# Graph network in one kernel: in stage two each eighth edge group, not each sixteenth, takes its fourth quarter from columns in SBUF instead of a gather

## The chip, the cores and the metric

One Trainium2 chip, one of its NeuronCores. The metric is the device time of one execution in microseconds (us); for the kernel before it is the median of three runs.

## The reference, cut to what matters

Two graph layers run over the same 200,000 edges (sorted by target `dst`) and 6,250 nodes of 128 features. The change lies in the second, an attention layer with 4 heads of 32 features:

```python
h = relu(layernorm(x))
x_l = (h @ W_l.T + b_l).reshape(n, 4, 32)
x_r = (h @ W_r.T + b_r).reshape(n, 4, 32)
z = leaky_relu(x_l[src] + x_r[dst], 0.2)
e = einsum('ehc,hc->eh', z, att)
e = exp(e - segment_max(e, dst)[dst])
alpha = e / (segment_sum(e, dst)[dst] + 1e-16)
out = segment_sum(alpha[:, :, None] * x_l[src], dst)
x = x + elu(out.reshape(n, 128) + bias)
```

Every edge needs the row `x_l[src]`. `dst` is sorted, `src` is random, so these rows have to be fetched one by one.

## The kernel before, in words

The edges are cut into 391 groups of 512 (`EG`), a group into four quarters of 128 edges (`J = 4`). Stage one (the message network, function `edges_mlp`) runs over all groups, then stage two (`edges_attention`) does. Each is a software pipeline written out by hand, with no scheduler: the five engines have programs of their own, tied by semaphores, and all go through the same slots. Eight slots are a round (`U = 8`), and slot g works at once on several groups of different age.

In slot g of stage two:

- TensorE turns the weights of group g-4 (L2466), multiplies the scores of g-2 (L2471, waits for `t_zt`), adds up the denominators of g-5 (L2476, L2477, wait for VectorE's `t_own_x`), then makes `z` of g-1 (L2496 for the target half, L2499 for the four quarters of source rows), and the weighted sum of g-4 (L2511, waits for ScalarE's `t_a_edge`).
- VectorE, in this order: its part of the columns (L931 loads the row numbers into registers, L935 copies), `t_zt` of g-2 (L2615), `t_own_x` of g-5 (L2620, waits for L2511 of the slot before), the logits of g-3 (L2627), `t_gap` and `t_drop` of g-5 (L2646 to L2653, wait for L2477 of this slot), the mask of g (L2663), and the accumulation of g-5 (L2669 to L2675, waits for ScalarE's `t_shrink`). Once a round come a few operations of a finished node tile, a reciprocal (L2180) among them.
- ScalarE: `t_a_edge` of g-4 (L2530, waits for L2466), `t_a_row` of g-3 (L2538), `t_shrink` (L2544), its part of the columns (L931, L2554), then `t_z` and `t_pen` of g-1 (L2558, L2560).
- GpSimd (POOL in the profile) issues the gathers, indirect DMAs of 128 rows from the table `tab_l` in HBM into `t_ring`, one a quarter (`gather_groups`, L1014). Before the gathers of group g it waits for TensorE: the first for the weighted sum of g-8, the next three for the turned weights, the `z` and the scores of groups some 4 to 7 back, all of which TensorE does near slot g-3. So GpSimd stays about four groups ahead of TensorE, and can't run further.
- SyncE loads the target windows and rows, and single rows for the lone groups.

Two kinds of group need no fourth gather. In each 32nd group (`lone`, g % 32 = 31) SyncE loads the 128 rows one by one, four a slot. In each 16th group (`chosen`, g % SPAN = 3, from g = 2 * SPAN on: 35, 51, ... 387, that is 23 groups) the rows come from `r.left`, the source features of all nodes, which lie transposed in SBUF. VectorE and ScalarE copy them a column at a time, 8 a slot (`CHOSEN = P // SPAN`), over the 16 slots that end two slots before slot g: four a slot by VectorE (`CHOSEN_BY_VECTOR`), the other four by ScalarE. SyncE fetches the list of row numbers ahead (`fetch_chosen`, L948). TensorE adds the 128 columns to `z` by a plain product with the identity (L2502, in place of a transpose), and turns them once more (L2495), from where ScalarE copies them to rows (L2537) for the weighted sum.

```python
    n, i = (g + SPAN - 2) // SPAN, (g - 2) % SPAN
    ...
    first += i * CHOSEN
    ...
    for q in range(many):
        last = move(r.chosen[n % 2][:, first + q:first + q + 1], r.left[:, bass.ds(rows[q], 1)])
```

Stage one has the same device under other names (`pick_columns`, L907, L911, L1750): there each eighth group has columns, eight a slot by either engine.

Of the kernel before, what the change touches and what calls it, by code (L numbers as in the profile page):

```python
# [32 lines left out]
PICKED = P // U  # L33
BY_VECTOR = 8
SOONER = 2
SPAN = 16
CHOSEN = P // SPAN
CHOSEN_BY_VECTOR = 4
LEAD = 5
SCALED = 2  # L40
FRONT = 2
# [7 lines left out]
def after(eng, sem, count):  # L49

    if isinstance(count, int) and count <= 0:
        return
    eng.wait_ge(sem, count)
# [12 lines left out]
def before(rnd, slot, k, tail):  # L66


    if tail and slot - k >= tail:
        return None  # L70
    slot -= k
    while slot < 0:
        slot += U
        rnd = rnd - 1
    if isinstance(rnd, int) and rnd < 0:
        return None
    return rnd, slot
# [804 lines left out]
def column(k, r, g, j):  # L882
# [3 lines left out]
    if j == J - 1 and chosen(k, g):  # L886
        return r.chosen_rows[g // SPAN % 2][:]
    return r.got[g % U][:, j, :]
# [26 lines left out]
def chosen(k, g):  # L915

    return g % SPAN == 3 and 2 * SPAN <= g < k.groups - 1


def choose_columns(nc, eng, k, r, s, g, first, many, move, done):  # L920

    n, i = (g + SPAN - 2) // SPAN, (g - 2) % SPAN
    if not many or not chosen(k, n * SPAN + 3):
        return
    if i == 0:
        if n == 2:
            eng.wait_ge(r.s_turned, 1)
        eng.wait_ge(r.s_chosen_ids, 16 * (n - 1))
        after(eng, s["t_zp"], (n - 2) * SPAN + 4 if n > 3 else 0)
    first += i * CHOSEN  # L930
    _, rows = nc.values_load_multi_w_load_instructions(  # L931
        r.chosen_ids[n % 2][:, first:first + many], engines=[eng.engine], min_val=0, max_val=k.N - 1,
        skip_runtime_bounds_check_because="src names rows of the node features, as the gathers take it")
    for q in range(many):
        last = move(r.chosen[n % 2][:, first + q:first + q + 1], r.left[:, bass.ds(rows[q], 1)])  # L935
    last.then_inc(done, 1)
# [1175 lines left out]
def edges_attention(nc, t, k, sems):  # L2112
# [3 lines left out]
    with ExitStack() as ctx:  # L2116
# [406 lines left out]
        def fast_scalar(act):  # L2523
            act.wait_ge(s["t_tiny"], 1)
            def body(rnd, slots, tail):
                for u in slots:
# [25 lines left out]
                    if not tail:  # L2552
                        choose_columns(nc, act, k, r, s, rnd * U + u, CHOSEN_BY_VECTOR, CHOSEN - CHOSEN_BY_VECTOR,
                                       lambda out, col: act.activation(out, col, ACT.Copy), r.s_chosen_s)  # L2554
# [19 lines left out]
        def fast_vector(dve):  # L2574
# [14 lines left out]
            def body(rnd, slots, tail):  # L2589
                for u in slots:  # L2590
# [19 lines left out]
                    if not tail:  # L2610
                        choose_columns(nc, dve, k, r, s, rnd * U + u, 0, CHOSEN_BY_VECTOR, dve.tensor_copy, r.s_chosen_v)
                    if at := before(rnd, u, 2, tail):
# [116 lines left out]
```

## Time and profile before

| | |
|---|---|
| median of 3 runs | 4867.06 us (4866.64 to 4870.92) |
| the profiled execution | 4868.36 us, span of its instructions 4865.6 us |
| stage one, about | 0 to 2430 us of the span |
| stage two, about | 2430 us to the end |
| busy, share of the span | PE 73%, PEld 57%, DVE 52%, ACT 46%, POOL 60% |
| mean granted TensorE clock | 0.79 of full speed |

A row of the timeline gives an instruction's start and duration, what it writes and reads, and in brackets how long its engine had been idle and what ended that. "remote" is a wait whose end the profile can't put down to an instruction, "issue" time in which the engine waited for nothing that the profile shows. PE is TensorE's matmul, PEld its weight load, DVE is VectorE, ACT ScalarE, POOL GpSimd; DVEq and ACTq are the instructions of their sequencers, as the loads of registers. A busy share is no bound by itself: no engine of this kernel is busy all the time, and what sets the length of a slot has to be read from the waits.

### The profile page before, as it was taken

Reading aid. Unit: us, or ns where it says so; the run is one execution under the profiler, and the core shown is the slowest. Engines: PE = TensorE matmul, PEld = TensorE weight load, DVE = VectorE, ACT = ScalarE, POOL = GpSimd, SP = SyncE. Lnnn points to the kernel's source line nnn. Section 1 sums busy time; section 2 is a strip of 40 time slices with the busy share of each in tenths; the row PEclk is TensorE's granted clock in tenths of the full one; section 3 lists DMA queues with packets and bytes.
Section 4 is the critical chain, followed back from the end, with each engine's and each line's share of the span. In section 5 each row is a group of like instructions: output and inputs, shape, how many; then the busy total and the mean of one; then the engine's idle time right before and its main releaser. Section 6 shows DMA issues by size and latency. Waiting matters only on the chain.

```text
span 4865.6 us, 90325 instructions
## 1 busy us (share of the span) xinstructions
PE 3546.4 (73%) x21208; PEld 2770.5 (57%) x21208; DVE 2514.7 (52%) x12768; ACT 2249.2 (46%) x8862; POOL 2910.5 (60%) x3098
## 2 busy tenths in 40 slices
PE   4778777888777778777757767667666666766766
PEld 3666666666666666666645555555545555555554
DVE  3444444444444444444436566666565665666665
ACT  3343444444444444444335555555555555555555
POOL 5666666666666666666466656666555665566564
PEclk7676767666766776777778889898898999889888
DMA  5344444444444444444322222222222222222221
GB/s 152 112 112 116 114 113 113 114 116 116 114 116 111 114 115 114 114 118 113 87 77 73 72 71 72 72 72 70 71 71 70 72 72 71 71 72 70 74 71 46
DMA packets 361802, 450.21 MB, mean 93 GB/s; under 512 B 163461, under 2 KB 217827, under 8 KB 361263
## 3 DMA queue, kind: packets, MB, share of 16 engines
q1 hardware_dynamic: 263359, 244.49, 17.6%
q0 software_dynamic: 97504, 199.69, 16.1%
q8 instruction: 174, 2.85, 0.2%
q14 instruction: 365, 2.99, 0.2%
q10 hardware_dynamic: 400, 0.20, 0.0%
HBM read 420.79 MB, written 23.28 MB: 91 GB/s over the span
## 4 chain that ended last, share of the span: by engine, by line
another core or an unknown queue 32%; DVE 23%; PE 20%; issue 14%; ACT 6%; DVEq 4%; DMA 0%; ACTq 0%; SPq 0%; POOL 0%; POOLq 0%
PE bank L2471 4%; DVE t_zt L2615 3%; DVE lone L911 3%; PE bank L2511 3%; PE bank L1694 3%; DVE m_pre L1793 2%; DVE t_logit L2627 2%; DVEq L907 2%; DVE t_chosen L935 2%; PE bank L2477 1%; PE bank L2499 1%; ACT t_a_row L2538 1%; PE bank L2466 1%; PE bank L2476 1%
## 5 line engine op out<-in xcount | busy, mean ns | idle before, releaser
L1014 POOL DMA_INDIRECT t_ring<-tab_l,src_t x1530 | 1446.1, 945 | 983.9 <-remote 447.3
L1014 POOL DMA_INDIRECT m_ring<-tab_a,src_t x1517 | 1440.3, 949 | 921.0 <-issue 387.3
L1694 PE MATMUL bank<-w,m_attr_t 128*128 128x128 f32 x3128 | 854.2, 399 | 128.1 <-issue 100.4
L1793 DVE TENSOR_TENSOR m_pre<-bank,m_ring 128x512 f32<-128x512 f32 (+1 forms) x391 | 264.0, 675 | 1168.4 <-remote 1078.3
L2471 PE MATMUL bank<-t_zt,att_wn 128*128 128x512 f32 x782 | 495.7, 719 | 499.3 <-issue 305.7
L1694 PEld LDWEIGHTS bank<-w,m_attr_t 128*128 128x128 f32 x3128 | 717.7, 280 | 233.3 <-issue 181.0
L1732 ACT ACTIVATE m_hid<-m_pre 128x512 f32<-128x512 f32 x391 | 245.8, 629 | 938.9 <-issue 663.7
L2530 ACT ACTIVATE t_a_edge<-bank 128x512 f32<-128x512 f32 x391 | 232.5, 595 | 699.4 <-remote 620.1
L2511 PE MATMUL bank<-t_ring,t_a_edge 128*128 128x128 f32 x3060 | 487.1, 310 | 64.6 <-issue 58.4
L2511 PEld LDWEIGHTS bank<-t_ring,t_a_edge 128*128 128x128 f32 x3060 | 448.3, 225 | 81.2 <-issue 73.9
L2471 PEld LDWEIGHTS bank<-t_zt,att_wn 128*128 128x128 f32 x782 | 132.7, 213 | 582.4 <-issue 359.2
L1699 PE MATMUL bank<-m_win,m_hot_t 96*128 96x128 bf16 x1564 | 430.5, 275 | 45.2 <-issue 44.9
L1682 PE MATMUL bank<-ident,m_ring 128*128 128x128 f32 x1564 | 363.1, 360 | 100.9 <-issue 90.8
L2476 PEld LDWEIGHTS bank<-diag_w,t_t_own_x 128*128 128x128 f32 x782 | 156.1, 218 | 446.7 <-issue 234.9
L1748 ACT ACTIVATE m_attr_t<-bank 128x512 f32<-128x512 f32 x391 | 230.2, 589 | 342.3 <-remote 264.6
L1662 PE MATMUL bank<-m_hid,m_hot 128*32 128x129 f32 x3128 | 208.1, 348 | 209.6 <-ACT m_hid L1732 119.1
L1682 PEld LDWEIGHTS bank<-ident,m_ring 128*128 128x128 f32 x1564 | 274.5, 196 | 126.6 <-issue 114.0
L2538 ACT ACTIVATE t_a_row<-t_logit,t_den_max 128x512 f32<-128x512 f32 x391 | 281.2, 719 | 104.9 <-DVE t_den_max L2627 73.3
L1750 ACT ACTIVATE lone<-HT 128x1 f32 x3008 | 323.3, 195 | 10.2 <-issue 3.5
L2615 DVE TENSOR_TENSOR t_zt<-bank,t_z 128x512 f32<-128x512 f32 x391 | 266.6, 682 | 51.7 <-issue 31.1
L2646 DVE TENSOR_TENSOR t_gap<-bank,HT 128x32 f32<-128x32 f32 x391 | 74.5, 191 | 408.7 <-PE bank L2477 194.4
L911 DVE COPY lone<-HT 128x1 f32 x3008 | 277.5, 145 | 8.2 <-issue 7.5
(276 smaller groups left out, 6756.1 us busy)
## 6 DMA issues: line engine op xcount, KB each, us to landing
m_ring<-in_edge_attr_dram SPq DMA_DIRECT2D x390, 256.0 KB
t_rows<-dst_rows SPq DMA_DIRECT2D x196, 256.0 KB
m_rows<-dst_rows SPq DMA_DIRECT2D x196, 192.0 KB
t_ring<-tab_l,src_t POOLq DMA_INDIRECT x1530
m_ring<-tab_a,src_t POOLq DMA_INDIRECT x1517
lone<-tab_l SPq DMA_DIRECT2D x1408, 0.5 KB
m_win<-tab_b SPq DMA_DIRECT2D x391, 24.0 KB
t_win<-tab_r SPq DMA_DIRECT2D x391, 24.0 KB
```

What stands on the lines that cost most here:

```text
L911: last = move(k.lone[:, n % 2, first + q:first + q + 1], k.HT[:, bass.ds(rows[q], 1)])
L1014: pool.indirect_dma_start(out=r.got[u][0:rows, j, :], out_offset=None, in_=table, in_offset=bass.IndirectOffsetOnAxis(ap=k.src_t[0:rows, g ...
L1682: last = pe.transpose(p_attr[u % 2][:, j * P:(j + 1) * P], attr[u][:, j, :], k.ident[:])
L1694: pe.matmul(p_hid[q % 2][:, e], lhsT=attr_t[q % 2][:, e], rhs=k.w1[:, 2, :], start=True, stop=False)
L1699: last = pe.matmul(p_hid[q % 2][:, e], lhsT=hot_t[q % 2][0:3 * W, e], rhs=r.win[q][:], start=False, stop=True)
L1732: act.activation(hid[q % 2][:, :, 0:P], pre[q % 2][:].rearrange("p (j d) -> p j d", d=P), ACT.Relu).then_inc(s["m_h"], 1)
L1750: lambda out, col: act.activation(out, col, ACT.Copy), s["m_picked_s"])
L1793: last = dve.tensor_tensor(pre[q % 2][:, 0:some], p_hid[q % 2][:, 0:some], r.got[q].rearrange("p j d -> p (j d)")[:, 0:some], ALU.add)
L2471: pe.matmul(p_e[q % 2][:], lhsT=k.att_wn[:], rhs=zt[q % 2][:], start=True, stop=True).then_inc(s["t_ep"], 1)
L2511: last = pe.matmul(p_nd[q % 2][:, 3 * W:3 * W + P], lhsT=a_edge[q % 2][:, j, :], rhs=column(k, r, g, j), start=(j == 0), stop=(j == J - 1))
L2538: act.activation(a_row[q % 2][:], logit[q % 2][:], ACT.Exp, scale=-1.0, bias=den_max[q % 4][:, 1:2], accum_out=den_max[q % 4][:, 0:1]).the ...
L2615: dve.tensor_tensor(zt[q % 2][:], p_z[q % 2][:], z02[q % 2][:], ALU.max).then_inc(s["t_z"], 1)
```

## The change

Two constants. `SPAN` goes from 16 to 8, so `CHOSEN`, the columns a slot, from 8 to 16, and VectorE's part from 4 to 7, ScalarE's from 4 to 9.

```diff
-SPAN = 16
+SPAN = 8
 CHOSEN = P // SPAN
-CHOSEN_BY_VECTOR = 4
+CHOSEN_BY_VECTOR = 7
```

The chosen groups are now 19, 27, ... 387, that is 47 of them, one in every round from round 2 on. The columns of one group are made over the 8 slots that end two slots before its own, so the slots that carry columns are 10 to 385 (376 slots), where they were 18 to 385 (368 slots). The two buffers of columns, of rows and of row numbers take turns as before, and SyncE fetches a list each 8 slots instead of each 16.

VectorE in stage two, in a slot that already had columns (t_chosen is the buffer of columns, X the features in SBUF, L935 ISA a register operation that goes with each copy, t_zt what TensorE's scores wait for):

```order
 L935 ISA
 L935 COPY t_chosen<-X 128x1
+L935 ISA
+L935 COPY t_chosen<-X 128x1
+L935 ISA
+L935 COPY t_chosen<-X 128x1
+L935 ISA
+L935 COPY t_chosen<-X 128x1
 L2615 TENSOR_TENSOR t_zt<-bank,t_z 128x512
 L2620 TENSOR_TENSOR t_t_own_x<-bank,same_head 128x128
```

Three more copies stand in each such slot ahead of `t_zt` and `t_own_x`, on which TensorE waits. ScalarE has five more at the like place, ahead of `t_z`.

TensorE in the slot that makes `z` of group 19, the first of the 24 groups that are new among the chosen ones. A group with four gathers, as group 19 was before:

```order
L2477 MATMUL bank<-t_cd,same_head 128x64
L2496 MATMUL bank<-t_hot_t,t_win 128x512
L2499 MATMUL bank<-ident,t_ring 128x128 x4
L2511 MATMUL bank<-t_ring,t_a_edge 128x128 x4
L2466 MATMUL bank<-ident,t_a_row 128x128 x4
```

and in the changed kernel:

```order
L2477 MATMUL bank<-t_cd,same_head 128x64
L2495 MATMUL bank<-ident,t_chosen 128x128
L2496 MATMUL bank<-t_hot_t,t_win 128x512
L2499 MATMUL bank<-ident,t_ring 128x128 x3
L2502 MATMUL bank<-t_chosen,ident 128x128
L2511 MATMUL bank<-t_ring,t_a_edge 128x128 x4
L2466 MATMUL bank<-ident,t_a_row 128x128 x4
```

One transpose of gathered rows has become a product with the columns, and one turn of the columns is added; the order is otherwise the same.

GpSimd's whole program for stage two, the difference (a row stands for so many gathers):

```order
 L1014 DMA m_ring<-tab_a,src_t 80x128 x4
-L1014 DMA t_ring<-tab_l,src_t 128x128 x1526
+L1014 DMA t_ring<-tab_l,src_t 128x128 x1502
 L1014 DMA t_ring<-tab_l,src_t 80x128 x4
```

24 gathers are gone, and nothing else has moved there.

## Rows read from the trace of the kernel before

**Rows 1.** Timeline of stage two, one slot with three gathers, all engines; start us, us

```profile
3037.74 0.29 DVE L2620 TENSOR_TENSOR t_t_own_x<-bank,same_head 128x128 f32<-128x128 f32 x1 [1.56 <-remote]
3037.80 0.60 ACT L2530 ACTIVATE t_a_edge<-bank 128x512 f32<-128x512 f32 x1 [2.13 <-remote]
3037.98 0.94 POOL L1014 DMA_INDIRECT t_ring<-tab_l,src_t  x1 [1.41 <-remote]
...
3038.88 0.19 DVE L2646 TENSOR_TENSOR t_gap<-bank,HT 128x32 f32<-128x32 f32 x1
...
3039.24 1.06 PE L2511 MATMUL bank<-t_ring,t_a_edge 128*128 128x128 f32 x8
...
3039.90 0.49 ACT L2554 ACTIVATE t_chosen<-X 128x1 f32 x4 [0.17 <-issue]
...
3040.13 0.60 PE L2466 MATMUL bank<-ident,t_a_row 128*128 128x128 f32 x4
...
3040.47 0.94 POOL L1014 DMA_INDIRECT t_ring<-tab_l,src_t  x1 [0.30 <-issue]
3040.74 0.50 DVE L935 COPY t_chosen<-X 128x1 f32 x4 [0.27 <-issue]
...
3041.15 0.68 DVE L2615 TENSOR_TENSOR t_zt<-bank,t_z 128x512 f32<-128x512 f32 x1
...
3042.70 0.29 DVE L2620 TENSOR_TENSOR t_t_own_x<-bank,same_head 128x128 f32<-128x128 f32 x1 [0.86 <-remote]
...
3042.93 0.94 POOL L1014 DMA_INDIRECT t_ring<-tab_l,src_t  x1 [1.51 <-remote]
```

**Rows 2.** Groups of instructions by line, 2550 to 4800 us; busy us, mean ns, idle before

```profile
L1014 POOL DMA_INDIRECT t_ring<-tab_l,src_t x1434 | 1355.5, 945 | 894.9 <-remote 426.7 <-issue 340.9 <-PE bank L2499 86.9
L2620 DVE TENSOR_TENSOR t_t_own_x<-bank,same_head 128x128 f32<-128x128 f32 x367 | 105.1, 286 | 313.1 <-remote 303.9 <-PE bank L2511 5.3 <-issue 3.2
L2646 DVE TENSOR_TENSOR t_gap<-bank,HT 128x32 f32<-128x32 f32 x367 | 69.9, 191 | 375.8 <-PE bank L2477 180.8 <-PE bank L2511 79.7 <-issue 72.2
```

**Rows 3.** Stretches, ten rounds of 32 gathers, first and sum; length, POOL busy

```profile
2693.20:2742.80 49.60, 29.33 (x32) 0.87 0.26 71
...
sum 502.20, POOL 303.83; mean POOL 30.38
```

**Rows 4.** Stretches, ten rounds each of the two kinds with one chosen group; sums

```profile
sum 487.00, POOL 288.15; mean POOL 28.82
...
sum 492.30, POOL 297.77; mean POOL 29.78
```

**Rows 5.** Instructions of single lines: columns, register loads, gathers; ns min/median/max

```profile
L935 DVE COPY t_chosen<-X x1472: 94/154/156, 2555.8 to 4808.9; 128x1 f32 x184
...
L931 DVEq TENSOR_LOAD <-w x192: 341/346/498, 2555.4 to 4808.1; - x192
L931 ACTq TENSOR_LOAD <-w x192: 306/311/358, 2561.2 to 4813.2; - x192
...
L907 DVEq TENSOR_LOAD <-wr x192: 593/596/812, 118.0 to 2375.6; - x192
L907 ACTq TENSOR_LOAD <-wr x192: 543/548/826, 122.0 to 2375.8; - x192
...
L1014 POOL DMA_INDIRECT t_ring<-tab_l,src_t x1500: 938/944/1076, 2449.6 to 4799.1; - x188
```

**Rows 6.** Stretches, three early rounds of 32 gathers: first and sum

```profile
2496.00:2545.50 49.50, 30.71 (x33) 0.84 0.27 70
...
sum 148.10, POOL 91.69; mean POOL 30.57
```

**Rows 7.** Timeline of DVE in stage two, where nothing is held

```profile
3018.15 0.68 DVE L2615 TENSOR_TENSOR t_zt<-bank,t_z 128x512 f32<-128x512 f32 x1
...
3020.53 0.19 DVE L2646 TENSOR_TENSOR t_gap<-bank,HT 128x32 f32<-128x32 f32 x1 [0.54 <-PE bank L2477]
```

## The prediction

> **What bounds the kernel now.** I read the page first (no engine is busy over 73% of the span, so no share names the bound), then the groups by line of stage two, then the timeline of single slots, then the lengths of whole rounds.
>
> In the groups by line, look at what stands behind each bar. GpSimd is busy 1355.5 us with 1434 gathers and idle 894.9 us; VectorE waits 313.1 us ahead of `t_own_x` and 375.8 us ahead of `t_gap` [rows 2]. All of them wait, and the rows name TensorE or nobody. The timeline shows how [rows 1]. `t_own_x` at 3042.70, and the next group's first gather at 3042.93, start within 0.25 us of one another, and at 3037.74, 3037.80 and 3037.98 they do so with ScalarE's `t_a_edge` too. What they wait for are matmuls of L2511 and L2466, which in this slot start at 3039.24 and 3040.13 and by their rows are over at 3040.30 and 3040.73. Yet nobody goes on until 3042.70, 2.2 us after the last gather of the group began at 3040.47. So TensorE's results, whose ends in a profile are only modelled, reach the others here when GpSimd has been quiet for a while. Whatever the cause, the slot has the shape: the gathers of a group at one pace, then one wait of everybody.
>
> The pace: a gather takes 0.945 us [rows 2] and the next follows 0.30 us later [rows 1], so 1.245 us. The wait: 1355.5 + 894.9 = 2250.4 us for 1434 gathers [rows 2], less 1434 x 1.245 = 1785, leaves 465 us over 367 slots, 1.27 us a slot. A slot of four gathers is then 4 x 1.245 + 1.27 = 6.25 us, one of three 5.0; the slot of the timeline, 3037.98 to 3042.93, took 4.95 [rows 1]. That is the main reading: **the number of gathers sets the length of a slot**, though their data are there long before they are needed.
>
> Whole rounds say it again. Ten rounds of 32 gathers took 502.2 us [rows 3], ten with one chosen group 487.0 and ten of the other kind with one 492.3 [rows 4]: 50.22 against a mean of 48.97, so 1.25 us for one gather less. In that difference the extra work of a chosen group (L2495, L2502, L2537) is paid already.
>
> **What it removes.** 24 gathers, at 1.245 us of pace each: 24 x 1.245 = 30 us, all on the path if the reading above holds. The rounds give 24 x 1.25 = 30 too. The added turns, products and copies to rows of the 24 new chosen groups are inside that number.
>
> **What it adds to VectorE.** Three copies a slot. Four take 0.50 us as a block [rows 1] and one 0.154 us [rows 5], so each further one adds (0.50 - 0.154) / 3 = 0.115, three 0.35 us. The load of row numbers is 346 ns for four and 596 ns for the eight of stage one [rows 5], so 63 ns a number, 0.19 us more, of which the engine sees all, since it already sits idle 0.27 us ahead of the block [rows 1]. Together 0.54 us a slot, and 376 x 0.54 = 203 us in all. The eight slots that had no columns get the whole block, some 1.4 us each, in rounds that are priced with the others.
>
> **What it adds to ScalarE.** Five copies at (0.49 - 0.19) / 3 = 0.10, 0.50 us, and five more numbers at (548 - 311) / 4 = 59 ns, 0.30 us [rows 1, 5]: up to 0.80 us a slot. It hides behind ScalarE's idle time ahead of `t_a_edge` (2.13 us at 3037.80) [rows 1]; what comes later by it is `t_z`, which VectorE takes a slot later. Priced at nothing; if the cover were gone, `t_a_edge` and with it L2511 would be late by up to 0.8 us.
>
> **What it adds elsewhere.** SyncE issues 24 more small fetches of numbers, and before each waits for the columns of the list before last, with the window loads of the next slots queued behind. It runs seven slots ahead of TensorE, and the columns it asks for are those of about the slot that TensorE is in, so this is a wait of under a slot against a lead of seven: nothing.
>
> **How much of VectorE's 0.54 us shows.** VectorE's chain runs through TensorE and back: `t_gap` at 3038.88 to the end of `t_zt` at 3041.83 is 2.95 us [rows 1]; from an end of `t_zt` (3018.83) to `t_gap` (3020.53) it is 1.70 where nothing is held [rows 7]. A slot of the chain alone is 4.65 us, with the change 5.19. Against 6.25 that hides; against a slot of three gathers, 4.95 to 5.0, it sticks out by some 0.2 us, and such slots will be 58 (47 chosen and 11 lone). Bounds: nothing, and all of it, 203 us. The nearest rows between are the early rounds of 32 gathers: the first, still without columns, took 49.5 us, the three together 148.1, so the two that have them 49.3 each [rows 6]. The later ones, with columns and the work on node tiles, took 50.22 [rows 3]. So 4 + 4 columns a slot, 8 x (0.50 + 0.27) = 6.2 us of VectorE a round, cost between nothing and 0.72 us a round, under 12% of what they take. At the same share the new 8 x 0.54 = 4.3 us a round cost 0 to 0.5 us, over 47 rounds 0 to 24. I take the middle, **12 us**; the 58 short slots at 0.2 us make the same.
>
> **The sum**: -30 + 12 = -18 us. The profiled execution took 4868.4 us, so 4850.4; the median of the runs is 1.3 us under it, so I forecast 4849.
>
> **A rule that speaks against it.** The copies of columns overlap gathers: the four from 3040.74 on lie inside the gather that began at 3040.47, and that one still took 0.94 us; over 1500 gathers the median is 944 and the longest 1076 ns [rows 5]. So the copies don't hold GpSimd up. The Trainium skill (SBUF — State Buffer, section "SBUF: two separate sides") states the opposite case: a VectorE copy of fp32 from SBUF to SBUF takes the port pair it shares with GpSimd, and the gather's descriptors can't be written meanwhile. By that rule each added copy would block a gather.
>
> **Rivals.**
>
> 1. *All of it hides.* For it: the early rounds, where columns cost nothing. Against: the short slots. Then -30: 4837 us. Chance 0.17.
> 2. *It cancels.* If the short slots are set by VectorE's chain with tile work in it (0.5 us instead of 0.2 in all 58, 29 us), the gathers' gain is given back: 4867 us, no change. Chance 0.15.
> 3. *Slower: a late result misses its gap.* TensorE's results get through when no gather is under way. In the short slot of each round, where the chain (5.19 us) is now longer than three gathers and the wait (5.0), L2511 or L2466 can come after GpSimd has started its next gather, and is then held for the length of one more, 1.245 us. Once a round that is 47 x 1.245 = 59 us, so -30 + 59 = +29: 4896 us. For it: the waits ahead of `t_gap` show that single results are held even now. Against: 0.2 us is little to miss by, and a slot late by that has a full slot of 6.25 us behind it to recover in. It decides from the point where 24 of the 47 rounds are hit. Chance 0.18.
> 4. *The copies block GpSimd after all.* Three copies of 0.154 us in 376 slots, one after the other on the gathers' path, are 174 us, so +144: 5011 us. Against it the rows above. Chance 0.02.
>
> That the change doesn't do what it says can be left out: the gathers in GpSimd's program went from 1526 to 1502.
>
> **How the numbers follow.** My forecast has 0.48. Single measurements of this kernel tell about 0.2%, 10 us, from no change. Of the forecast's own spread (0 to 24 us of cost around 12, so 4837 to 4861) some 0.07 falls inside 10 us of no change. Faster: 0.41 + 0.17 = 0.58. Same: 0.07 + 0.15 = 0.22. Slower: 0.18 + 0.02 = 0.20. The range takes in full hiding with a few us to spare, 4833, and reaches into rival 3 with fewer rounds hit, 4885; beyond it lie the rest of rival 3, rival 4 and a little on the fast side, some 0.2. The likeliest case alone has 4837 to 4861.
>
> **What would show it.** Gathers in stage two 1506 (1530 before), copies on L935 2632 (1472 before), on L2554 3384. Rounds with one chosen group of about 49 to 49.5 us, and none left at 50.2; slots of three gathers 5.0 to 5.5 us. The idle time ahead of `t_own_x` and `t_gap` should be less by some 0.5 us a slot in all, since the copies eat it; GpSimd's wait should stay near 1.27 us a slot. Wrong would be: rounds with a chosen group no shorter than 50 (rival 2 or 3), with GpSimd's wait grown to 1.5 us a slot and more, or gathers longer than 0.95 us in the mean (rival 4). If the rounds are 49.0 as before, rival 1 holds.

## The result and the profile after

The changed kernel takes **5189.69 us** (median of 4 runs, 5184.25 to 5191.47) against 4866.85 us (4 runs). The ratio is 1.0662, with an interval of 1.0645 to 1.0679: 323 us slower, where 18 us faster was forecast. The profiled execution took 5189.53 us, with a span of 5187.7 us. The whole loss lies in stage two: its first gather starts at 2432.6 us of the span, and at 2433.2 before.

The counts are the forecast ones: 1506 gathers in stage two, 2632 copies on L935, 3384 on L2554. The single lines show what is not. The columns are instruction, count, then minimum, median and maximum in ns, then first and last start:

```profile
L935 DVE COPY t_chosen<-X x2632: 153/154/156, 2507.2 to 5128.2; 128x1 f32 x188
...
L931 DVEq TENSOR_LOAD <-w x192: 1030/1040/1100, 2506.0 to 5126.3; - x192
L931 ACTq TENSOR_LOAD <-w x192: 1947/1959/2099, 2510.9 to 5133.6; - x192
...
L907 DVEq TENSOR_LOAD <-wr x192: 593/597/753, 118.6 to 2375.4; - x192
L907 ACTq TENSOR_LOAD <-wr x192: 537/548/857, 121.2 to 2375.6; - x192
```

VectorE's load of seven numbers takes 1040 ns and ScalarE's of nine 1959, where four took 346 and 311 [rows 5]. Yet eight numbers, in stage one of the same kernel, still take 597 and 548. Seven cost more than eight.

The groups by line of stage two, 2550 to 4800 us as in [rows 2]. In the kernel before, ScalarE's `t_a_edge` had this row:

```profile
L2530 ACT ACTIVATE t_a_edge<-bank 128x512 f32<-128x512 f32 x367 | 218.3, 595 | 667.0 <-remote 595.9 <-PE bank L2466 58.1 <-issue 12.7
```

and in the changed kernel:

```profile
L1014 POOL DMA_INDIRECT t_ring<-tab_l,src_t x1238 | 1171.6, 946 | 1079.6 <-PE bank L2499 667.6 <-issue 297.3 <-PE bank L2502 93.9
...
L2554 ACT ACTIVATE t_chosen<-X 128x1 f32 x2889 | 319.8, 193 | 574.4 <-issue 574.4
...
L2530 ACT ACTIVATE t_a_edge<-bank 128x512 f32<-128x512 f32 x322 | 188.8, 586 | 0.4 <-remote 0.4
...
L2620 DVE TENSOR_TENSOR t_t_own_x<-bank,same_head 128x128 f32<-128x128 f32 x322 | 90.4, 281 | 0.2 <-remote 0.2
...
L2646 DVE TENSOR_TENSOR t_gap<-bank,HT 128x32 f32<-128x32 f32 x322 | 61.7, 192 | 357.7 <-PE bank L2477 271.4 <-issue 84.0 <-PE bank L2511 2.3
```

2250 us now hold 322 slots, 6.99 us each, and not 367 of 6.13 [rows 2]. The 0.86 us times 376 slots are 323 us, the whole loss. GpSimd's wait, reckoned as in the prediction, is (1171.6 + 1079.6 - 1238 x 1.246) / 322 = 2.20 us a slot and not 1.27; it has a name now, L2499, TensorE's `z`, so GpSimd waits for a late TensorE. The wait ahead of `t_own_x`, 313.1 us before, is gone, and so is ScalarE's ahead of `t_a_edge`: 0.4 us, where it was 667.0. ScalarE instead waits 574.4 us ahead of its columns, for "issue", that is for its own sequencer, which is loading registers. The gathers' mean is 0.946 us, as before.

Ten rounds with one chosen group each, first and sum. The columns are the length of the stretch, the busy us (and count) of PE, PEld, DVE, ACT and POOL, then the granted clock, the DMA share and GB/s:

```profile
2737.98:2794.31 56.33, 35.25 (x200) 27.40 (x200) 33.27 (x172) 30.58 (x127) 29.32 (x31) 0.89 0.24 63
...
sum 568.84, PE 365.06 PEld 282.74 DVE 328.32 ACT 302.30 POOL 291.42; mean PE 36.51 PEld 28.27 DVE 32.83 ACT 30.23 POOL 29.14
```

56.9 us a round, against 48.7 and 49.2 [rows 4], with the same number of gathers. The timeline of one slot shows why (start, duration, engine; the idle time before it in brackets):

```profile
3036.60 0.58 ACT L2558 ACTIVATE t_z<-bank 128x512 f32<-128x512 f32 x1
...
3037.21 0.69 DVE L2615 TENSOR_TENSOR t_zt<-bank,t_z 128x512 f32<-128x512 f32 x1
...
3037.96 1.12 PE L2471 MATMUL bank<-t_zt,att_wn 128*128 128x512 f32 x2 [2.91 <-issue]
...
3039.06 0.41 PE L2477 MATMUL bank<-t_cd,same_head 128*128 128x64 f32 x2
...
3039.61 0.19 DVE L2646 TENSOR_TENSOR t_gap<-bank,HT 128x32 f32<-128x32 f32 x1 [0.76 <-issue]
...
3040.13 0.26 ACT L2544 ACTIVATE t_shrink<-t_drop 128x64 f32<-128x64 f32 x1 [0.58 <-DVE t_drop L2653]
3040.40 0.95 POOL L1014 DMA_INDIRECT t_ring<-tab_l,src_t  x1 [1.72 <-PE bank L2499]
...
3042.08 0.84 DVE L935 COPY t_chosen<-X 128x1 f32 x7 [0.95 <-issue]
3042.20 0.98 ACT L2554 ACTIVATE t_chosen<-X 128x1 f32 x9 [1.81 <-issue]
...
3043.09 0.58 ACT L2558 ACTIVATE t_z<-bank 128x512 f32<-128x512 f32 x1
...
3043.70 0.69 DVE L2615 TENSOR_TENSOR t_zt<-bank,t_z 128x512 f32<-128x512 f32 x1 [0.79 <-ACT t_z L2558]
```

Read it as a ring, a closed chain of waits that sets the length of a slot, from `t_z` to `t_z`: to `t_zt` 0.61 us, to L2471 0.75, to L2477 behind it in TensorE's order 1.10, to `t_gap` 0.55, to `t_shrink` 0.52, then ScalarE's load, up to its first column, 2.07, and its columns 0.89. That is 6.49 us from 3036.60 to 3043.09, and no gather stands in it. It is one of the shortest slots: from `t_zt` to `t_zt` those between 2800 and 3400 us take 6.48 us and more, in the mean 7.1; in the longer ones more comes on top (work on node tiles, a lower granted clock), which was not taken apart. Before, in the slot of [rows 1]:

```profile
3039.47 0.26 ACT L2544 ACTIVATE t_shrink<-t_drop 128x64 f32<-128x64 f32 x1
...
3040.30 0.58 ACT L2558 ACTIVATE t_z<-bank 128x512 f32<-128x512 f32 x1
```

So `t_shrink` to the first column (3039.90 [rows 1]) took 0.43 us, and the columns 0.40. The two last terms grew by 2.1 us, of which the old common wait of 1.27 us took up a part, and 0.86 us came out at the end.

### The profile page after: what moved, and what is told of

It reads as the page before. It is cut to its first block, busy times and chain, and to the rows that moved or that the text cites. A ratio compares the mean times of both kernels' runs of the same rounds, so it can differ in the third digit from the quotient of the medians.

```text
span 5187.7 us, 96749 instructions
## 1 busy us (share of the span) xinstructions
PE 3622.0 (70%) x21256; PEld 2874.7 (55%) x21256; DVE 2664.8 (51%) x13928; ACT 2442.5 (47%) x10798; POOL 2893.4 (56%) x3074
## 4 chain that ended last, share of the span: by engine, by line
PE 32%; issue 23%; another core or an unknown queue 21%; DVE 15%; DVEq 4%; ACT 4%; ACTq 1%; DMA 0%; SPq 0%; POOL 0%
PE bank L2471 9%; PE bank L2511 5%; PE bank L1694 3%; DVE lone L911 3%; PE bank L2499 3%; PE bank L2477 2%; PE bank L2466 2%; DVE m_pre L1793 2%; DVE t_zt L2615 2%; DVEq L907 1%; DVEq L931 1%; PE bank L2496 1%; PE bank L2476 1%; ACTq L931 1%
## 5 line engine op out<-in xcount | busy, mean ns | idle before, releaser
L1014 POOL DMA_INDIRECT t_ring<-tab_l,src_t x1506 | 1425.4, 946 | 1324.5 <-PE bank L2499 780.6
L2471 PE MATMUL bank<-t_zt,att_wn 128*128 128x512 f32 x782 | 532.1, 768 | 979.7 <-issue 727.4
L2471 PEld LDWEIGHTS bank<-t_zt,att_wn 128*128 128x128 f32 x782 | 133.4, 214 | 1076.5 <-issue 793.1
L2554 ACT ACTIVATE t_chosen<-X 128x1 f32 x3384 | 374.8, 193 | 673.7 <-issue 673.7
L2511 PE MATMUL bank<-t_ring,t_a_edge 128*128 128x128 f32 x3012 | 506.3, 323 | 3.9 <-ACT t_a_edge L2530 2.3
L935 DVE COPY t_chosen<-X 128x1 f32 x2632 | 317.6, 154 | 324.3 <-issue 319.8
L2511 PEld LDWEIGHTS bank<-t_ring,t_a_edge 128*128 128x128 f32 x3012 | 477.4, 240 | 4.8 <-ACT t_a_edge L2530 2.7
L2476 PEld LDWEIGHTS bank<-diag_w,t_t_own_x 128*128 128x128 f32 x782 | 179.2, 230 | 244.6 <-issue 238.1
```

The lines of the kernel that those rows point to most:

```text
L1014: pool.indirect_dma_start(out=r.got[u][0:rows, j, :], out_offset=None, in_=table, in_offset=bass.IndirectOffsetOnAxis(ap=k.src_t[0:rows, g ...
L2471: pe.matmul(p_e[q % 2][:], lhsT=k.att_wn[:], rhs=zt[q % 2][:], start=True, stop=True).then_inc(s["t_ep"], 1)
L2511: last = pe.matmul(p_nd[q % 2][:, 3 * W:3 * W + P], lhsT=a_edge[q % 2][:, j, :], rhs=column(k, r, g, j), start=(j == 0), stop=(j == J - 1))
```

## The experiments

The kernel before takes a very different time on different chips: 4802 us on the chip of e1 to e4 (mean granted clock of TensorE 0.80), 3910 on that of e5 to e8, 3911 on that of e9 to e12, 3917 for e13 to e16 (all three 0.89), 4858 for e17 and e18 (0.79). So each result is a ratio to the kernel before on the same chip. Where a difference is taken across chips, the text says so; e5 to e8 and e9 to e12 are such a case, with 0.3 us between their kernels before.

### e1: what a register load costs

The kernel before, with another length and first place of the load in each of the 16 slots between two chosen groups:

```diff
-    _, rows = nc.values_load_multi_w_load_instructions(
-        r.chosen_ids[n % 2][:, first:first + many], ...
+    if vector is True and i == 0:
+        _, rows = nc.values_load_multi_w_load_instructions(ids[:, first - 0:first + 4], ...
+    elif vector is True and i == 1:
+        _, rows = nc.values_load_multi_w_load_instructions(ids[:, first - 0:first + 5], ...
...
+    elif vector is True and i == 12:
+        _, rows = nc.values_load_multi_w_load_instructions(ids[:, first - 1:first + 7], ...
```

> The kernel before (each sixteenth group, four and four columns), but in stage two each slot's register load on VectorE and on ScalarE has another length and first place: on VectorE 4 to 14 and 16 numbers from a place divisible by eight, and 8, 8, 8 and 7 numbers from places that are not; on ScalarE 4 to 10, 12 and 13 numbers from places 0, 1, 4 or 7 of eight. Only the numbers that were used before are used. Theory A (the load's time follows the count of numbers in steps, and not in a straight line): 4 and 8 numbers take some 0.33 and 0.57 us wherever they start, 7 and 9 numbers some 1.04 and 1.96 us. Theory B (the place of the first number decides): 7 and 9 numbers from a place divisible by four take below 0.7 us, 8 numbers from place 1, 6 or 7 take over 1 us. The prediction's straight line (about 60 ns a number) would have 7 at 0.52 and 9 at 0.65 us, whatever the place. The run's own time should be some per cent above the kernel before by A, about the same by the straight line.

Measured: 4882.9 us in a single run against 4801.8, 1.7% more. In order: VectorE with 4, 5, 7, 8, 9, 12 and 16 numbers from a place divisible by eight, 8 from place 4, 7 and 8 from place 7; then ScalarE with nine from place 0, nine from place 7 (what the change does), and nine from place 4.

```profile
L934 DVEq TENSOR_LOAD <-w x12: 346/352/355, 2533.5 to 4730.2; - x12
L937 DVEq TENSOR_LOAD <-w x12: 601/608/612, 2540.8 to 4737.0; - x12
L943 DVEq TENSOR_LOAD <-w x12: 1030/1040/1050, 2553.0 to 4748.2; - x12
L946 DVEq TENSOR_LOAD <-w x12: 601/606/611, 2558.4 to 4753.9; - x12
L949 DVEq TENSOR_LOAD <-w x12: 851/853/856, 2566.0 to 4761.0; - x12
L958 DVEq TENSOR_LOAD <-w x12: 853/856/892, 2583.9 to 4780.5; - x12
L967 DVEq TENSOR_LOAD <-w x12: 1104/1108/1116, 2603.7 to 4797.6; - x12
L973 DVEq TENSOR_LOAD <-w x12: 594/596/601, 2616.4 to 4809.5; - x12
L976 DVEq TENSOR_LOAD <-w x12: 1632/1635/1652, 2622.4 to 4814.9; - x12
L970 DVEq TENSOR_LOAD <-w x12: 1853/1854/1868, 2610.3 to 4803.4; - x12
```

```profile
L988 ACTq TENSOR_LOAD <-w x12: 786/788/794, 2551.8 to 4747.0; - x12
L991 ACTq TENSOR_LOAD <-w x12: 1981/1989/1998, 2557.6 to 4752.7; - x12
L1021 ACTq TENSOR_LOAD <-w x12: 773/776/782, 2621.6 to 4814.0; - x12
```

The times fit a load that, if its first place is divisible by four, reads four numbers at once as long as four are left and the rest singly, and that otherwise reads every number singly. Four, eight, 12 and 16 numbers are 352, 606, 856 and 1108 ns, some 250 for each further four; the fifth alone costs as much as four more (608), and each single one after it some 215 (seven: 1040). From place 7, which is not divisible by four, nothing goes in fours: seven are 1635 and eight 1854 ns. So theory A was half right: the count decides, but the place does too. ScalarE's nine would have cost 0.78 us from place 0 or 4; because VectorE has seven they begin at place 7, and cost 1.99. The Trainium skill (Runtime: NRT & Kernel Launch, section "Instruction fetch mechanics") gives about 200 ns a register, even in bulk, for loads from HBM; these are from SBUF. The single reads come near it (1854 / 8 = 232 ns), the reads of four lie far below it (1108 / 16 = 69 ns).

### e2 to e4: short loads with the copies, long loads without them

Edits to the changed kernel: `CHOSEN_BY_VECTOR = 8` (e2); seven and nine kept, but VectorE loads eight numbers and ScalarE one and then eight (e3). Edit to the kernel before (e4):

```diff
+    a, b = (first, first + 7) if first % CHOSEN == 0 else (first - 1, first + 8)
+    a = min(a, P - (b - a))
-        r.chosen_ids[n % 2][:, first:first + many], ...
+        r.chosen_ids[n % 2][:, a:a + (7 if first % CHOSEN == 0 else 9)], ...
+    rows = rows[first - a:]
```

> The changed kernel with eight columns a slot by VectorE and eight by ScalarE in place of seven and nine. The gathers and the sum of the copies are as in the changed kernel. Theory A (the loads of 7 and 9 numbers are the loss): both loads fall to about 0.57 us as stage one's loads of eight do, ScalarE's idle time before t_a_edge comes back, and the time falls from 5190 to 4830 to 4880 us. Theory C (the eight more copies a slot themselves, 0.8 us over two engines, or SyncE's doubled fetches, make the loss): the time stays within 5130 to 5200 us. Theory D (the late result misses its gap between two gathers): GpSimd's wait stays near 1.8 us a slot and the time near 5190 us even with short loads.

> The changed kernel with its seven and nine columns, but VectorE loads eight numbers and uses seven, and ScalarE loads one number and then eight, in two loads. All copies are the changed kernel's. Theory A: VectorE's load about 0.57 us instead of 1.04, ScalarE's two about 0.25 and 0.57 us instead of 1.96 together, so the time falls to 4850 to 4920 us. Theory C (copies or fetches): stays at 5190 us within 1%. A theory by which each load has a fixed price that two loads pay twice: ScalarE's pair is above 1.2 us and the time above 4950 us.

> The kernel before (each sixteenth group, four and four columns), but its loads take seven numbers on VectorE and nine on ScalarE, of which the four of before are used. No copy, gather or fetch is added. Theory A: the loads take 1.04 and 1.96 us, the loop through ScalarE has the changed kernel's length less five copies (some 0.5 us) a slot, so 4980 to 5120 us. Theory C: 4867 us within 0.5%, since ScalarE's idle time before t_a_edge hides the loads.

Measured, on a chip with 4801.8 us before: e2 4975.3 us, ratio 1.0371 (1.0347 to 1.0395); e3 4965.4 us, 1.0359 (1.0324 to 1.0394); e4 4989.5 us, 1.0393 (1.0372 to 1.0413). The loads were as short as expected (0.60 and 0.55 us in e2). e4 shows that the long loads alone, with no copy, gather or fetch added, cost 188 us:

```profile
L2533 ACT ACTIVATE t_a_edge<-bank 128x512 f32<-128x512 f32 x329 | 192.8, 586 | 5.4 <-remote 4.5 <-PE bank L2469 0.6
...
L2557 ACT ACTIVATE t_chosen<-X 128x1 f32 x1312 | 164.3, 194 | 580.1 <-issue 580.1
```

In its groups by line (2550 to 4700 us) the cover ahead of `t_a_edge` is gone and the sequencer's wait has its place, as in the changed kernel. But e2 and e3 came out well above theory A's 4830 to 4880 and 4850 to 4920 us: short loads took the ratio from 1.066 (another chip) only to 1.037. The long loads are a part of the cause and not the whole. What is left in e2 stands on VectorE: `t_zt` sits idle for 1.5 us in 337 slots (2550 to 4700 us), 0.7 of it for `t_z`, so VectorE comes to `t_zt` last, after its load and eight copies. Two short loads in e3 cost no more than one in e2.

### e5 to e7: the parts one by one

e5 is the kernel before with every load taking eight numbers; e6 has its short loads but copies every column twice, first into a tile that nobody reads; e7 is the changed kernel with `CHOSEN_BY_VECTOR = 4`, so twelve by ScalarE.

```diff
-        r.chosen_ids[n % 2][:, first:first + many], ...
+        r.chosen_ids[n % 2][:, first - first % 8:first - first % 8 + 8], ...
```

```diff
-    for q in range(many):
-        last = move(r.chosen[n % 2][:, first + q:first + q + 1], r.left[:, bass.ds(rows[q], 1)])
+    for to in (r.spare, r.chosen):
+        for q in range(many):
+            last = move(to[n % 2][:, first + q:first + q + 1], r.left[:, bass.ds(rows[q], 1)])
```

> The kernel before (each sixteenth group, four and four columns), but every load takes the eight numbers of its slot, from a place divisible by eight: 0.60 us on VectorE and 0.55 us on ScalarE by the ladder, 0.25 and 0.23 us more than the kernel before. Theory E (before, VectorE's part of a slot has no slack, so that work added ahead of t_zt lengthens nearly each slot): 0.15 to 0.25 us a slot over 376 slots, 55 to 95 us, a ratio of 1.012 to 1.020. Theory F (the eight and eight version is slow by its copies or its fetches): a ratio within 0.3% of 1.

> The kernel before with its short loads of four numbers, but each column is copied twice (once into a tile that nobody reads): eight copies a slot on VectorE and eight on ScalarE, some 0.4 us more on each, no fetch and no gather changed. Theory E: 0.3 to 0.4 us a slot, 110 to 150 us, a ratio of 1.023 to 1.032. Theory F by the copies: the whole of the eight and eight version's loss and the lost gathers' 30 us, a ratio of 1.037 to 1.045. Theory G (only the loads, at the sequencer, cannot be hidden, while copies are): within 0.5% of 1.

> Each eighth group, with four columns a slot by VectorE (as before the change) and twelve by ScalarE, whose load of twelve numbers takes 0.78 us by the ladder. VectorE's work is that of the kernel before. Theory E (VectorE's part has no slack, ScalarE's has some 1.8 us of idle time before t_a_edge, against 0.46 us of load and 0.8 us of copies added): about the kernel before or faster, a ratio of 0.99 to 1.01. Rival H (ScalarE's work ahead of t_z is in the same loop, since t_zt waits for t_z): a ratio of 1.04 to 1.08, worse than eight and eight.

Measured, before 3910.4 us: e5 3964.9, ratio 1.0142 (1.0125 to 1.0159); e6 3973.5, 1.0163 (1.0146 to 1.0180); e7 4288.1, 1.0967 (1.0948 to 1.0985). A quarter microsecond of load shows (54.5 us, 0.15 a slot), as theory E had it, and 0.4 us of copies show (63 us, 0.17 a slot), if less than it expected. e7 refutes the other half of theory E, that ScalarE has room: with VectorE's work untouched, ScalarE's 1.27 us more (0.47 of load, 0.80 of columns) cost 378 us, 1.00 a slot. Rival H had the place right and the size too small (a ratio of 1.04 to 1.08). What `t_zt` waits for says it too (2400 to 3600 us of e7):

```profile
L2615 DVE TENSOR_TENSOR t_zt<-bank,t_z 128x512 f32<-128x512 f32 x203 | 140.3, 691 | 161.2 <-ACT t_z L2558 161.0
```

So ScalarE's idle time ahead of `t_a_edge`, in which the prediction had hidden them, does not cover what stands ahead of `t_z`.

### e8: the first try at moving the loads

The changed kernel, with ScalarE's load ahead of its wait for `t_drop` (the columns stay), and VectorE's load and columns between `t_zt` and `t_own_x`.

> The changed kernel with its seven and nine columns and its loads of seven and nine numbers, moved: ScalarE's load stands ahead of the wait for t_drop (its columns stay), and VectorE's load and columns stand ahead of the wait for own_x's product, where each engine waits for others in the kernel before. Nothing is left out. Theory A (exposed loads): ScalarE's load of 1.96 us then fills a wait of some 1.0 us and shows by 0 to 1 us instead of 1.8, VectorE's 1.04 us is mostly hidden: a ratio of 0.99 to 1.03 in place of 1.066. If the place of the loads does not matter, the ratio stays near 1.06.

Measured: 4572.2 us, 1.1692 (1.1673 to 1.1712), hardly better than the changed kernel on a chip with the same time before (e9, 1.1853). `t_shrink` stands in the ring, so a load ahead of it costs about as much as one behind it. VectorE's block was moved in the same run, so e8 doesn't tell the two moves apart. The expectation took each idle time for a cover without asking what the engine would do next.

### e9 to e12: out of the ring

From this and the timeline came theory L: the ring goes `t_z`, `t_zt`, L2471, `t_gap`, `t_shrink` and ScalarE's load and columns. The one long wait of ScalarE off it is that for `t_den_max`, behind `t_a_edge`. (As the steps above go, the part from L2471 to `t_shrink` runs through VectorE's `t_gap`; the expectations name `t_logit` and `t_a_row` for it.) e9 is the changed kernel; e10, e11 and e12 have this edit on it, on eight and eight, and on the kernel before:

```diff
@@ fast_scalar, in each slot: from ahead of t_z to behind t_a_edge
+                    if not tail:
+                        choose_columns(nc, act, k, r, s, rnd * U + u, CHOSEN_BY_VECTOR, ...
                     if at := before(rnd, u, 3, tail):
...
@@ fast_vector: from ahead of t_zt to behind it
+                    if not tail:
+                        choose_columns(nc, dve, k, r, s, rnd * U + u, 0, CHOSEN_BY_VECTOR, ...
                     if at := before(rnd, u, 5, tail):
```

> The changed kernel as it is, as the yardstick for the runs beside it, since chips differ in the TensorE clock they grant (the kernel before took 4867, 4802 and 3910 us on three). On a chip with a clock near 0.8 a ratio of 1.06 to 1.08; on one near 0.89 1.10 to 1.15, since the kernel before waits there only for its gathers and the changed one for the loop of t_z, t_zt, L2471, t_logit, t_a_row, t_shrink, ScalarE's load and its columns.

> The changed kernel with its seven and nine columns and its loads of 7 and 9 numbers, both as long as ever (1.04 and 1.96 us), but in other places: ScalarE's load and columns between t_a_edge and the wait for t_den_max, VectorE's between t_zt and the wait for the attention product. Theory L (ScalarE's load and columns stand in the loop t_z, t_zt, L2471, t_logit, t_a_row, t_shrink, t_z; out of it they cost nothing up to the wait for t_den_max, some 1.8 us): the load of 1.96 us and nine columns of 0.93 us are 1.1 us longer than that wait, so a ratio of 0.99 to 1.04. Theory A alone (a long load costs wherever it stands): above 1.05.

> Each eighth group with eight and eight columns, loads of 0.60 and 0.55 us, in the places of the run before this. Theory L: 0.55 us and eight columns of 0.85 us fit in ScalarE's wait of 1.8 us, so the loop is shorter than the kernel before's by its load and four columns (0.7 us) and GpSimd's gathers bound the slot again; 24 or more fewer gathers at 1.245 us: a ratio of 0.95 to 0.995, faster than the kernel before. If the copies cost by themselves wherever they stand: above 1.02.

> The kernel before (each sixteenth group, four and four) with the loads and columns in the new places. Theory L: the loop loses 0.3 us of load and four columns of 0.45 us: a ratio of 0.96 to 1.0, on a chip of a clock near 0.8 more than on a fast one; the difference to eight and eight in the new places is then the price of the gathers, 24 x 1.245 us = 30 us, 0.6%, with eight and eight the faster.

| | us | ratio | interval |
|---|---|---|---|
| before | 3910.7 | | |
| e9 changed | 4635.1 | 1.1853 | 1.1833 to 1.1873 |
| e10 changed, moved | 3952.3 | 1.0122 | 1.0094 to 1.0151 |
| e11 eight and eight, moved | 3880.6 | 0.9924 | 0.9908 to 0.9941 |
| e12 before, moved | 3911.4 | 1.0002 | 0.9992 to 1.0011 |

e9 lost more than expected (1.10 to 1.15); e10 and e11 came out within theory L's ranges, and e12 at their edge. The move alone takes 683 us off the changed kernel, with the same loads (1.04 and 1.97 us) and copies. With eight and eight the kernel is 30.1 us faster than before and 30.8 faster than e12. That is the prediction's term: 24 gathers at 1.245 us are 30. The stretches of e11 say that the gathers set the pace (columns as in the ten rounds above), and the group by line that almost all of GpSimd's idle time is its own issue time (2400 to 3600 us):

```profile
2800.00:3200.00 400.00, 327.94 (x1942) 237.31 (x1943) 337.24 (x1819) 309.94 (x1207) 302.76 (x320) 0.97 0.35 90
3200.00:3600.00 400.00, 326.09 (x1942) 233.95 (x1942) 337.50 (x1824) 309.38 (x1209) 302.67 (x320) 0.97 0.34 90
```

```profile
L1014 POOL DMA_INDIRECT t_ring<-tab_l,src_t x958 | 908.3, 948 | 292.1 <-issue 256.7 <-PE bank L2499 20.1 <-PE bank L2466 7.0
```

320 gathers in 400 us are 1.25 us each, with 0.30 of issue between them and almost no wait. e9 makes 226 in the same 400 us. The ring's arithmetic, an estimate across two chips, comes out for e9 as well: e7 showed that 1.27 us of ScalarE's work cost 1.00, so some 0.27 are free; the change adds 1.65 of load and 0.50 of columns there, less 0.27 is 1.88 a slot, and 724 us over 376 slots are 1.93.

In e10 the load of nine still shows a little: behind `t_a_edge` the columns wait 1.53 us for it, and `t_a_row` stands behind them.

```profile
3039.01 0.58 ACT L2530 ACTIVATE t_a_edge<-bank 128x512 f32<-128x512 f32 x1
3041.13 0.98 ACT L2534 ACTIVATE t_chosen<-X 128x1 f32 x9 [1.53 <-issue]
...
3042.17 0.71 ACT L2541 ACTIVATE t_a_row<-t_logit,t_den_max 128x512 f32<-128x512 f32 x1
```

### e13 to e16: which engine

e13 moves only ScalarE's load and columns in the changed kernel, e14 only VectorE's; e15 is eight and eight in the old places, e16 in the new ones.

> The changed kernel (seven and nine), ScalarE's load and columns moved between t_a_edge and the wait for t_den_max, VectorE's left ahead of t_zt. Theory L (ScalarE's share is in the loop, VectorE's runs beside it): nearly all of the loss goes, a ratio of 1.01 to 1.04. If VectorE's 1.04 us and seven columns ahead of t_zt make the loop by themselves: within 0.02 of the changed kernel.

> The changed kernel (seven and nine), VectorE's load and columns moved behind t_zt, ScalarE's left ahead of t_z. Theory L: nothing or little is won, a ratio within 0.02 of the changed kernel (1.066 on a chip of clock 0.79, 1.185 on one of 0.89), perhaps worse, as VectorE's share then stands between t_zt and t_logit. If VectorE's share was the loss: near 1.01.

> Each eighth group with eight and eight columns in the old places, again. On a chip of a clock near 0.8: 1.037 as before. On one near 0.89, by theory L: the loop is 1.41 us of load and 0.1 of a column shorter than the changed kernel's, whose slot there is near 6.9 us against 4.97 of before, so 5.3 to 5.6 us, a ratio of 1.03 to 1.06.

> Eight and eight in the new places, again. By theory L 0.992 on a chip of a clock near 0.89 (the gathers' 30 us alone), and 0.95 to 0.995 on one near 0.8, where the kernel before waits for its loop in part of its slots.

Measured, before 3917.5 us: e13 4483.0, ratio 1.1438 (1.1415 to 1.1462); e14 4933.2, 1.2597 (1.2576 to 1.2618); e15 4177.6, 1.0665 (1.0648 to 1.0683); e16 3886.1, 0.9920 (0.9903 to 0.9936). Three expectations missed. Theory L had e13 at 1.01 to 1.04, e14 within 0.02 of the changed kernel's 1.185 ("perhaps worse"), and e15 at 1.03 to 1.06. It was too narrow: ScalarE's share alone is not nearly all of the loss, since VectorE's makes a second ring that is almost as long. The timeline of e13, then the wait ahead of `t_zt` in e13 and in e15 (2400 to 3600 us):

```profile
3039.73 0.26 ACT L2547 ACTIVATE t_shrink<-t_drop 128x64 f32<-128x64 f32 x1 [0.58 <-DVE t_drop L2653]
...
3040.50 0.22 DVE L2675 TENSOR_TENSOR acc<-t_old,t_new 128x64 f32 x1
...
3041.68 0.84 DVE L935 COPY t_chosen<-X 128x1 f32 x7 [0.96 <-issue]
3042.43 0.68 DVE L2615 TENSOR_TENSOR t_zt<-bank,t_z 128x512 f32<-128x512 f32 x1
```

```profile
L2615 DVE TENSOR_TENSOR t_zt<-bank,t_z 128x512 f32<-128x512 f32 x188 | 128.0, 681 | 0.5 <-issue 0.5
```

```profile
L2615 DVE TENSOR_TENSOR t_zt<-bank,t_z 128x512 f32<-128x512 f32 x214 | 145.6, 680 | 0.0
```

From `t_shrink` the way goes through the accumulation, VectorE's load and its seven columns to `t_zt`, 2.70 us. In neither run does `t_zt` wait for `t_z`, so it is VectorE's ring that sets the slot there, with short loads (e15) even while ScalarE's block stands in its old place. With ScalarE's long load in the old place it is `t_zt` that waits for `t_z`, by 0.79 us in the changed kernel's slot. e15 has 0.71 us more of VectorE's work a slot than before (0.25 of load, 0.46 of copies) and loses 260 us, 0.69 a slot. e13 has 1.04 us more, 391 us in all, and loses 566: its slots between 2800 and 3400 us are 5.61 us at the shortest, as that ring has it, but 6.40 in the mean. The longer ones go with a lower granted clock (see the last section). Taking one of two parallel ways out leaves the other. Moving VectorE's alone, e14, makes it worse: its load and columns then stand between `t_zt` and `t_own_x`, in series with ScalarE's (`t_zt` at 3042.25, `t_own_x` at 3044.19). e15 against e16 is the clean pair for short loads: 291 us for nothing but the place of the block.

### e17 and e18: how far it goes

e17 is e11 with `SPAN = 4` and sixteen and sixteen columns a slot, e18 is e11 again.

> Each fourth group chosen, sixteen columns a slot by VectorE and sixteen by ScalarE, in the new places; some 48 gathers fewer than with each eighth, worth 60 us or 1.5% if the gathers still bound the slot. Their loads take 1.11 us on VectorE by the ladder and some 1.05 on ScalarE, the columns some 1.8 and 1.6 us. Theory L: ScalarE's 2.6 us are longer than the wait for t_den_max of some 1.8 us, and VectorE's 2.9 us longer than its wait for the attention product, so the loop grows by 1 us or more: a ratio of 1.03 to 1.12. If both still hid: 0.975 to 0.98.

> Eight and eight in the new places once more. On a chip where the kernel before takes 4800 us or more: 0.93 to 0.99; on one where it takes 3910 us: 0.992 again.

Measured, before 4858.4 us: e17 5355.5, ratio 1.1022 (1.1004 to 1.1041), as expected from blocks longer than the waits that should hide them; e18 4852.4, 0.9987 (0.9978 to 0.9997), 6 us faster and only just clear of no change. The expectation for e18 missed: of the gathers' 30 us a fifth arrived. Its groups, 2550 to 4700 us:

```profile
L1014 POOL DMA_INDIRECT t_ring<-tab_l,src_t x1354 | 1283.2, 948 | 867.8 <-remote 340.3 <-issue 327.9 <-PE bank L2499 153.0
...
L2620 DVE TENSOR_TENSOR t_t_own_x<-bank,same_head 128x128 f32<-128x128 f32 x352 | 100.1, 284 | 139.2 <-remote 138.1 <-issue 0.8
```

The common wait with no name ("remote") is there as on the chip of the prediction's trace [rows 2]: (1283.2 + 867.8 - 1354 x 1.248) / 353 = 1.31 us a slot, a little more than its 1.27. In the groups of e11 and e12 (chip of 3911 us) no wait has that name. What ends it, and why fewer gathers shorten a slot less where it exists, stays open; no run took it apart, and e12 was not run on such a chip.

## Why the prediction was wrong

**The failed steps** are the prices of what is added, and how much of it was taken to hide. Under "What it adds to ScalarE", five more numbers were priced at 59 ns each and the whole "at nothing", since it "hides behind ScalarE's idle time ahead of `t_a_edge`". Both halves are wrong.

- *The price of a load.* A straight line was drawn through four and eight numbers, the two counts that divide by four. ScalarE's load was to go from 0.31 to 0.61 us and went to 1.96; VectorE's was to take 0.54 and took 1.04 (e1). With the columns, ScalarE's 0.80 us a slot was 2.15. With short loads in their place the ratio falls from 1.185 (e9) to 1.067 (e15, another chip, with 7 us between their kernels before): roughly two thirds of the loss there. On the chips near 4800 us it was less, 1.066 against 1.037 (e2).
- *The cover.* The columns stand ahead of `t_z`, and `t_zt` waits for `t_z`. Idle time behind them, ahead of `t_a_edge`, hides nothing of them. The prediction wrote the right sentence ("what comes later by it is `t_z`, which VectorE takes a slot later") and stopped there, though its chain ends in that very `t_zt`. With VectorE's work untouched, 1.27 us more on ScalarE cost 1.00 a slot (e7); moving both blocks away, with the same loads and copies, took 683 us off (e10 against e9).
- *VectorE's 0.54 us a slot* was 1.04, the load's 0.69 and the copies' 0.35. As the sum went, the chain would have been 5.69 us, not 5.19. The chain itself was read rightly: it is the second ring, and e13's shortest slots take 5.61 us.
- *How much of it shows.* "Under 12%" was taken over from the early rounds. On a chip like that of the prediction's trace, e2 adds 0.71 us to VectorE, 267 us in all, and loses 173 even with the gathers' gain in it: two thirds or more show. On the faster chips nearly all does: 260 us in e15, which gains 31 once the blocks are moved (e16). The chain was held against mean slots of 6.25 and 5.0 us, but the single slots of the kernel before vary from 4.6 to 8.9 us (`t_zt` to `t_zt`, 2800 to 3400 us), and a mean says nothing of those that the chain binds. Why so much shows on the slow chips stays open.

**The gathers' term** was right where the gathers bound the slot: 24 x 1.245 = 30 us, measured as 30.1 and 31.3 us (e11, e16, chips near 3911 us). On a chip like that of the prediction's trace only 6 us came out (e18), and no run shows the full 30 there. **The reading of what bounds the kernel** was not safe, though. The common wait was taken for a fixed addend of 1.27 us, with results that get out only when GpSimd is quiet. In e11 and e12 gathers follow one another without a pause and all engines go on, and in the changed kernel the wait for nobody ahead of `t_own_x` is 0.2 us. The rows fit slack that the added work uses up first, until the ring lies bare; that is argued and not shown, since what makes the wait stays open (e18).

**The rivals.** Rival 1, all hides, has the result of e11 and e16, at other places and lengths. Rival 3, a result that misses its gap, is not what happened: slots of four gathers grew as well, and moving the block healed them. Rival 4, copies that block GpSimd, is refuted: eight VectorE copies a slot run in e11 with gathers of 0.948 us, against 0.945 before [rows 2]. The Trainium skill's rule (SBUF — State Buffer, section "SBUF: two separate sides") does not show for these single columns. No rival had a load at two to three times its price, and none reached 5190 us.

**The signs named beforehand** pointed right: rounds longer than 50 us and GpSimd's wait above 1.5 us a slot were to refute the forecast, and they read 56.9 and 2.20. SyncE's added fetches, priced at nothing, are in e11 too and do no harm.

## What to carry to other kernels

An idle time covers added work only if that work stands on the way to nothing else: follow what is queued behind it on its engine, and close the ring before calling it hidden. A price between two measured points can be far off, as that of seven numbers between four and eight; choose counts and first places of register loads that divide by four. When two engines share a block of work, both ways through it must be taken off the ring together (e10), since either alone leaves the other or makes it worse (e13, e14).

## What the hardware showed that was not expected

- A register load on VectorE takes 352 ns for four numbers, 606 for eight and 1040 for seven; 1854 for eight from place 7 (e1). ScalarE's behave alike (nine: 788 ns from place 0, 1989 from place 7). The Trainium skill (DMA: Bandwidth & Descriptors, section "Latency and other measured facts") states a floor of some 600 ns for `tensor_load`; four numbers in 306 to 352 ns here lie below it.
- A register load can start while its engine still works on the instruction before: in the changed kernel's slot the first column starts 1.81 us after `t_shrink` ends, less than the load's 1.96. Of a long load 1.5 (e10) to 1.8 us show as idle time.
- Chips gave the kernel before 3910 to 4867 us. TensorE's mean granted clock was 0.89 on the fast ones and 0.79 to 0.80 on the others; no run shows that this alone makes the difference. The clock was also lower in slower kernels on one chip or like chips: 0.89 before and 0.84 in e9, 0.89 before and 0.78 in e14. A lower clock lengthens the ring: in e13 two L2471 matmuls of 512 columns took 1.12 us in one slot and 1.44 in the next, and the clock of the stretches around them was 1.00 (full speed, 2.4 GHz; 3030 to 3040 us) and 0.83 (3040 to 3050 us). How much of each loss is the clock's own share was not measured apart.
